# Where the softmax epilogue of an attention pair stands in the issue order, and which PSUM banks its broadcast uses

## The reference

```python
x = x + 0.5 * ffn(layernorm(x))
x = x + attn(layernorm(x))
x = x + 0.5 * ffn(layernorm(x))

# inside attn, per head (hd = 64, L = 32):
att = einsum('bhql,bhkl->bhqk', q_for_k, k_lat) * L ** (-0.5)
att = where(causal, att, -inf)
att = softmax(att, axis=-1)
y_lat = einsum('bhqk,bhkl->bhql', att, v_lat)
y = y_lat @ l2o_w.T + l2o_b
return y @ cproj_w.T + cproj_b
```

## Time and profile before

| | |
|---|---|
| time, median of 2 runs | 5588.74 us (5555.71 and 5621.76) |
| the profiled execution | 5548.91 us |
| its span, slowest core (core 1) | 5547.4 us; the cores lie between 5484.7 and 5547.4 |
| PE matmul busy | 3706.4 us (67%) |
| DVE busy | 1938.5 us (35%) |
| ACT busy | 1671.7 us (30%) |
| largest group on ACT | L877, the exponentials, 1254.8 us |
| largest groups on PE | L904 (PV) 890.1 us, L865 (S) 760.8 us |
| shares of the chain that ended last | PE 49%, DVE 15%, issue 15%, ACT 10%, DMA 5% |

### The profile page before, as it was taken

One profiled execution on the slowest core, in us unless ns is written; L12 is line 12 of the kernel. 1 busy time (PEld: TensorE's weight loads), 2 busy tenths in 40 slices (PEclk: granted clock), 3 DMA queues, 4 the chain that ended last, 5 costly groups with the idle time before them and its releaser, 6 DMA issues.

```text
span 5547.4 us, 58481 instructions; the slowest of 8 cores (5484.7 to 5547.4 us)
## 1 busy us (share of the span) xinstructions
PE 3706.4 (67%) x13322; PEld 1162.8 (21%) x13322; DVE 1938.5 (35%) x4078; ACT 1671.7 (30%) x1938; POOL 698.3 (13%) x884
## 2 busy tenths in 40 slices
PE   0117666677876676677776667667786667677887
PEld 0002212222221222122221222122221222122222
DVE  1115432541124533451133533363123543353113
ACT  0000350027620062006740044005750035003662
POOL 0002002200013101310003100310003200320001
PEclk9997657776577856786676766678877766777567
DMA  2242103210022102210013101310003100321002
GB/s 88 66 139 61 31 3 105 64 46 1 1 65 91 54 8 65 89 52 12 1 31 110 57 20 31 110 53 24 1 20 112 57 29 10 116 61 31 1 1 80
DMA packets 152518, 277.12 MB, mean 50 GB/s; under 512 B 34322, under 2 KB 34322, under 8 KB 152210
## 3 DMA queue, kind: packets, MB, share of 16 engines
q1 hardware_dynamic: 124818, 210.44, 12.8%
q0 software_dynamic: 8960, 29.37, 1.8%
q10 hardware_dynamic: 18432, 33.56, 1.6%
HBM read 231.36 MB, written 46.14 MB: 50 GB/s over the span
## 4 chain that ended last, share of the span: by engine, by line
PE 49%; DVE 15%; issue 15%; ACT 10%; DMA 5%; POOL 3%; SPq 1%; DVEq 1%; ACTq 0%; POOLq 0%
PE PS L904 13%; PE PS L865 10%; PE PS L620 9%; PE PS L690 7%; ACT PT L877 5%; PE PS L1000 5%; DVE ln_sb L602 3%; DMA stg<-w_attn 3%; DVE rb_sb L952 3%; ACT r_sb L925 2%; POOL sq_sb L558 1%; PE PS L568 1%; PE PS L563 1%; PE PS L799 1%; DVE t_sb L713 1%
## 5 line engine op out<-in xcount | busy, mean ns | idle before, releaser
L877 ACT ACTIVATE PT<-PS,b_exp 128x1024 bf16<-128x1024 f32 (+7 forms) x1536 | 1254.8, 863 | 594.5 <-PE PS L865 567.0
L904 PE MATMUL PS<-PT,v_store 128*65 128x512 bf16 (+3 forms) x2560 | 890.1, 467 | 22.0 <-DVE PT L883 13.4
L865 PE MATMUL PS<-q_store,k_store 32*128 32x512 bf16 (+3 forms) x2560 | 760.8, 460 | 197.6 <-DVE rb_sb L952 110.0
L620 PE MATMUL PS<-ln_sb,wslot 128*128 128x512 bf16 x2048 | 665.5, 466 | 158.6 <-DVE ln_sb L606 120.4
L883 DVE TENSOR_TENSOR PT<-PT,causal_sb 128x128 bf16<-128x128 bf16 x1024 | 230.4, 225 | 1440.6 <-ACT PT L877 1432.2
L690 PE MATMUL PS<-ln_sb,wslot 128*128 128x512 bf16 x2048 | 635.7, 457 | 82.0 <-DVE ln_sb L606 82.0
L555 POOL CAST xb_sb<-x_sb 128x512 bf16<-128x512 f32 x384 | 243.7, 635 | 3464.4 <-DVE x_sb L1010 2638.3
L575 ACT ACTIVATE m_bf<-PS 1x512 bf16<-1x512 f32 x48 | 28.1, 586 | 1838.8 <-PE PS L563 1808.8
L558 POOL TENSOR_TENSOR sq_sb<-xb_sb 128x512 bf16<-128x512 bf16 x384 | 399.2, 1040 | 881.1 <-PE PS L568 822.0
L904 PEld LDWEIGHTS PS<-PT,v_store 128*65 128x65 bf16 x2560 | 297.0, 135 | 532.5 <-issue 453.3
L865 PEld LDWEIGHTS PS<-q_store,k_store 32*128 32x128 bf16 x2560 | 172.9, 97 | 785.8 <-issue 767.1
(11 more groups left out here) (103 smaller groups left out, 2321.3 us busy)
## 6 DMA issues: line engine op xcount, KB each, us to landing
wslot<-me_strm SPq DMA_DIRECT2D x256, 256.0 KB, 2.6
wslot<-wa_strm SPq DMA_DIRECT2D x256, 256.0 KB, 2.6
wslot<-cp_strm SPq DMA_DIRECT2D x128, 256.0 KB, 2.6
out<-stg ACTq DMA_DIRECT2D x128, 256.0 KB, 3.0
x_sb<-x POOLq DMA_DIRECT2D x112, 256.0 KB, 4.2
stg<-w_attn SPq DMA_DIRECT2D x48, 256.0 KB
x_sb<-x SPq DMA_DIRECT2D x8, 512.0 KB
wa_strm<-build_sb SPq DMA_DIRECT2D x16, 256.0 KB
```

Of the source, the lines that this page charges most:

```text
L620: fns.append(lambda eng, j=j, dd=dd, bk=bk: eng.matmul(bank_ap(bk, 0, TTA), slot_ap(j, dd), ln_sb[:, TTA * dd:TTA * dd + TTA], start=(dd = ...
L865: hg=hg, gq=gq: eng.matmul(PS[:, 1024 * par + a:1024 * par + bnd], k_store[32 * hg:32 * hg + 32, seq * gq + 128 * c:seq * gq + 128 * c + 128],
L877: eng.activation(PT[:, QW * slot + qoff:QW * slot + QW], PS[:, 1024 * par + qoff:1024 * par + QW], AF.Exp, bias=b_exp[:, 0:1]),
L904: yb=yb: eng.matmul(PS[0:65, yb + a:yb + bnd], v_store[:, 1040 * c + 65 * h:1040 * c + 65 * h + 65], PT[:, QW * slot + a:QW * slot + bnd], ...
```

## The change

Three things change, all of them at the pair boundary.

1. The epilogue of the finished pair is emitted behind the S of chunk 1 of the next pair and not behind that of chunk 0.
2. E writes to partitions 64 to 127 of the y banks of its own head (4, 5 and 6, 7) and not to partitions 0 to 63 of the S banks (0, 1 and 2, 3). Row 64, the softmax sum, has been read by then.
3. The copy reads from there: partitions 64 to 127 in, partitions 0 to 63 of `rb_sb` out.

The number of instructions, their shapes and the multiply do not change. The TensorE stream becomes S(h0,0), S(h1,0), S(h0,1), S(h1,1), E0, E1, PV(h0,0), PV(h1,0), S(h0,2), ...; on DVE the causal multiplies of chunk 1 (hb = 0) now stand ahead of copy0.

```diff
--- before.py
+++ after.py
@@ -912,7 +912,7 @@
         for c in range(nchunks):
             s_chunk(h0, c)
             s_chunk(h0 + 1, c)
-            if c == 0 and defer_in is not None:
+            if c == min(1, nchunks - 1) and defer_in is not None:
                 defer_in()
                 defer_in = None
             if c >= 1:
@@ -937,21 +937,19 @@
             ybanks = [BK[4 + 2 * par]] + ([BK[5 + 2 * par]] if QW > 512 else [])
 
             def epilogue(h=h, yb=yb, ybanks=ybanks, par=par):
-                rb0 = 1024 * par
-                rbanks2 = [BK[2 * par]] + ([BK[2 * par + 1]] if QW > 512 else [])
-                p.group("tensor", [lambda eng, rb0=rb0, par=par: eng.matmul(
-                    PS[0:64, rb0:rb0 + min(512, QW)], ones1x_sb[0:1, 0:64],
+                p.group("tensor", [lambda eng, yb=yb, par=par: eng.matmul(
+                    PS[64:128, yb:yb + min(512, QW)], ones1x_sb[0:1, 0:64],
                     r_bf[:, QW * par:QW * par + min(512, QW)],
                     start=True, stop=True)] +
-                    ([lambda eng, rb0=rb0, par=par: eng.matmul(
-                        PS[0:64, rb0 + 512:rb0 + QW], ones1x_sb[0:1, 0:64],
+                    ([lambda eng, yb=yb, par=par: eng.matmul(
+                        PS[64:128, yb + 512:yb + QW], ones1x_sb[0:1, 0:64],
                         r_bf[:, QW * par + 512:QW * par + QW],
                         start=True, stop=True)] if QW > 512 else []),
                     reads=[p.R("rbf", par), p.R("ones1x")],
-                    writes=rbanks2)
-                p.op("vector", lambda eng, rb0=rb0, par=par: eng.tensor_copy(
-                    rb_sb[:, QW * par:QW * par + QW], PS[0:64, rb0:rb0 + QW]),
-                    reads=rbanks2, writes=[p.R("rb", par)])
+                    writes=ybanks)
+                p.op("vector", lambda eng, yb=yb, par=par: eng.tensor_copy(
+                    rb_sb[:, QW * par:QW * par + QW], PS[64:128, yb:yb + QW]),
+                    reads=ybanks, writes=[p.R("rb", par)])
                 hp, sub = h // 2, h % 2
                 p.op("vector", lambda eng, hp=hp, sub=sub, yb=yb, par=par:
                      eng.tensor_tensor(
```

## The result

The changed kernel takes 5655.21 us (median of 11 runs), the kernel before, over 10 runs, 5539.54 us. The ratio is 1.0215 with a 95% interval of 1.0181 to 1.025. That is about 119 us slower (the two medians differ by 116), and whether it is more or less than 2% the interval leaves open. The slowest of the ten runs of before, 5621.76 us, fell in a slower state of the chip and is left out of the ratio. The two runs of before that stood ahead of the prediction lie in the upper part of the ten (5516.33 to 5621.76).

What follows compares the result with a forecast made beforehand. The prediction took the boundary path (exponential, E0, copy0 to copy1, S(h1,1), PV, S(h0,2)) as the bound, hardly any of it ACT's. Steps of 39 + 53 = +92 us on the median 5588.74 gave 5681 us, range 5605 to 5755.

Steps and rivals of the forecast that it cites:

- The order as the path: Pair boundary: PV waits for the multiply, 112 times, some 2 and 1.5 us; S(h0,2) stands behind PV of the second head.
- The sizes at the boundary: S(h0,2) starts later at each pair boundary: +1.40 us for hb = 1, +1.89 us for hb = 0.
- priced at zero: Copy in the epilogue: reading other partitions than it writes was taken to cost zero; a dearer copy wasn't excluded.
- The open bound: Boundary of hb = 1: E0 might run beside S(h1,1), making the step +0.46 us; the forecast took one behind the other.
- The lower bound of 66 us: Sum over all boundaries if E0 overlaps S(h1,1): 28 x 0.46 + 53 = +66 us.
- The sum: All boundaries: 28 x 1.40 + 28 x 1.89 = 39 + 53 = +92 us, clock mix unchanged; chance 0.57.
- rival B: Pairs after the boundary: clock rises later or not at all, +194 us to 5783, half of it 5732; chance 0.25.
- the mix: Pairs of both halves: shares of pairs with early and late clock rises assumed the same as before, adding nothing.
- The absolute time: Whole kernel: the median shown, 5588.74 us, plus 92 gives 5681 us.
- A: ACT at the boundary: it runs ahead and its two gaps are saved, -244 us, to 5345; chance 0.05.
- C: TensorE at the boundary: the unbroken run S, S, E0, E1 raises the clock earlier, -8 us, to 5581; chance 0.13.
- The pair that the prediction calls fully busy: Pair of hb = 1, 40.53 busy of 47.70 us at clock 0.57, cited to show being busy isn't enough to raise it.

Runs made afterwards that it cites:

- E0: Not a run: the E matmul of the first head in the epilogue, on TensorE; no kernel e0 was run, so it has no ratio.
- e6: Changed kernel with PV one chunk later in the order and a third P tile per head; ratio to the kernel before 1.0009.
- e3: Changed kernel with the copy of the second head on ACT instead of DVE; ratio to the kernel before 1.0039.
- e2: Kernel before with E in the y banks and the copy reading there, epilogue still behind S of chunk 0; ratio to the kernel before 0.9956.
- e1: Kernel before with only the epilogue moved behind S of chunk 1, E still in the S banks; ratio to the kernel before 1.0253.
- e5: Changed kernel with ten further matmuls, results never read, in TensorE's idle time behind S of chunk 0; ratio to the kernel before 1.0204.
- e9: Kernel before with the copy of the second head done twice, order unchanged; ratio to the kernel before 1.0142.
- e4: Kernel before with the y banks and the copy of the second head on ACT, epilogue at its old place; ratio to the kernel before 0.9801.
- e8: As e4, but the causal multiply of chunk 0 stands behind the epilogue's DVE work of its head; ratio to the kernel before 0.9786.

## Why the prediction was right

**The order as the path.** Right in each step. PV waits for the multiply (L955 in the changed kernel, the prediction's L957) 112 times; in the boundary shown by 1.95 and 1.55 us (forecast "some 2 and 1.5"). PV of the second head holds S(h0,2) and everything behind it; e6 shows that by taking it out, e3 by shortening the chain ahead of it.

**The sizes at the boundary.** Forecast +1.40 (hb = 1) and +1.89 (hb = 0), measured +1.50 and +1.93. The tenth in hb = 1 is made of small terms: E0 came 0.11 sooner than worked out (3.20 behind the first exponential, forecast 3.31), but copy0 to the end of multiply1 took 5.13 and not 4.99, the copy began 0.03 later behind E0, and PV of the second head took 0.97 and not 0.93. The 0.14 of the chain comes from where the copy reads, which I had priced at zero: the copy itself is 14 ns longer,

```profile
L950 DVE CAST rb_sb<-PS x128: 1225/1226/1227, 661.5 to 5548.9; 64x1024 bf16<-64x1024 f32 x128
```

against 1212 in the earlier trace rows, and copy1 starts 1.25 behind multiply0, before 1.14. As means over the boundaries of hb = 1 the chain takes 5.13 us in the changed kernel and in e2, 5.02 before and in e1, so it goes with the banks and partitions and not with the place. Banks and partitions changed together in all runs, and which of the two it is stays open.

**The open bound.** E0 does not run beside S(h1,1): the row of four S matmuls lasts 2.01 us from 1271.93, the last two of them take 1.01, so S(h1,1) starts at 1272.93 and E0 0.95 behind it, as PV had behind S (0.94). The lower bound of 66 us is out. The Trainium skill's rule that a change of tiling mode drains TensorE ("TensorEngine Tiling (Array Packing)", Tiling Modes, Key Properties) agrees, but E and S have other rows and other columns at once, so no run here shows that the mode is the reason.

**The sum.** Steps of 28 x 1.50 + 28 x 1.93 = 96 us against the forecast 92. The measured 119 of the stages hold 23 more: some 5 between S(h0,2) and S(h0,3), and 18 behind S(h0,3), nearly all of these in hb = 0 (16 us), where the granted clock is 0.56 and was 0.71. That is rival B in part: the mix that the forecast had taken as unchanged got worse there. B as written, all pairs at the low rate, holds for 176 of the 224 pairs of hb = 0 (clock 0.50 all the way behind S(h0,3), before 71 of 224) and not for hb = 1. So the term that was mis-sized is the clock's, put at 0 and measured at 18, and it lifted the ratio from the 1.017 of the forecast to about 2% (1.0181 to 1.025). The forecast had given 0.60 to a change within 2% and 0.35 to one slower than that; the runs don't decide between the two.

**The absolute time.** 5681 was forecast, 5655 measured, though the step was too small: the median that I scaled to, of two runs, lay 49 us above that of ten (the slowest of the ten is one of the two). The two errors nearly cancel; that the absolute time came so close is luck.

**The rivals.** A: ACT did get its work early and idled 7.25 us for it; no gain. C: the run of S, S, E0, E1 did not raise the clock. From the first exponential to S(h0,2) it is 0.50 in all 448 boundaries of the changed kernel, as it was before. The fillers of e5 did raise it (above), and it didn't pay. The rule of the Trainium skill that sustained matmul work raises the clock ("TensorE: Matmul & The Clock Gate", Part 1) agrees with the fillers, but here it was no guide to how long a pair takes. The pair that the prediction calls fully busy was busy for 40.53 of its 47.70 us; the stretch without a gap is this one inside that pair, kernel before, with the clock at 0.50:

```profile
5166.00:5180.00 14.00, 14.00 (x36) 0.50 0.00 0
```

**What stays open.** Why the pairs of hb = 0 lose the early rises. Lateness alone isn't it (e9). The kernels with a clock of 0.57 or less behind S(h0,3) are the changed one, e1, e4 and e8, and e4 and e8 have the shortest boundaries of those with PV early. I found no single feature that these four have and the others lack. One difference does show in the clock of the traces: a rise less than 2 us behind S(h0,2). The kernel before has it in 68 of its 448 boundaries and e9 in 148; all the others have it in none. Before and e9 are the kernels in which TensorE works without a gap from S(h1,1) over the four PV matmuls to S(h0,2); in the others it waits between the PV matmuls of the two heads, or PV comes later. That fits the idea that the broken work loses the early rises, but the later rises differ too, and no run tests it by itself. In the same way the pairs of hb = 1 took back 1.1 us of the 1.5 gained in e2, and 0.35 of 2.8 in e4.

## What to carry to other kernels

When an epilogue is moved later in a hand-written order, list what its buffers hold up on the engine's own queue: here TensorE's queue had stood at S of chunk 1, until the second head's copy was through, and now stands at PV, until the second head's multiply is through, one DVE instruction further down a chain that also starts later. Giving the epilogue banks of its own and moving it are two changes, and they should be measured apart: the first gained, the second lost more. Where the clock of TensorE goes up and down within a stage, work the step out inside the boundary, compare it there over all cores, and leave room for the mix: for steps of 50 to 122 us, the mean span came out 18 to 34 us away from their sum here (changed, e2, e4, e9).

## What was not expected of the hardware

- A copy out of partitions 64 to 127 of PSUM into partitions 0 to 63 took 1226 ns, out of partitions 0 to 63 1212; and the next copy began 0.11 us later behind the multiply. The banks differed as well.
- The same 64 x 1024 copy out of partitions 64 to 127 took ACT 1.02 us and DVE 1.23.
- A boundary shorter by 50 us in sum (e2) shortened the mean span by 16 us, one longer by 73 us (e9) lengthened it by 100, one shorter by 122 (e4) by 104. (As means over all runs, against the runs of before made with them: 10, 96 and 95.) The granted clock behind the boundary ranged over 0.56 to 0.79 (hb = 0) and 0.77 to 0.85 (hb = 1) in kernels that there run the same instructions (PV later left out).
- Matmuls into rows that nobody reads raised the granted clock at the boundary, to 1.00 in 439 of 448 boundaries, and in every one it was at 0.50 again from PV to S(h0,2).
- In the kernel before, the granted clock behind S(h0,3) of hb = 0 takes three values, 0.50, about 0.70 and 0.90 to 0.94, in 71, 75 and 78 pairs; in the changed kernel the same three, in 176, 30 and 18.
